# Attention and expert kernel on one Trainium2 core: the score exponential's factor, the engine that sends the maxima's rows, and a new plan

## The chip, the cores and the metric

The kernel runs on one core of a Trainium2 chip. The metric is the device time of one execution in microseconds (us); the time before is the median of three executions. The engines are TensorE (PE; its weight loads are PEld), VectorE (DVE), ScalarE (ACT), GpSimd (POOL) and SyncE (SP, which here only issues transfers).

## The reference, cut to what matters

```python
def attention(q, k, v, mask, ...):                  # q = layernorm(x), k = v = ctx
    qh, kh, vh = (heads(t @ W + b) for ...)         # 8 batches, 512 tokens, 16 heads of 32
    sim = einsum('bnid,bnjd->bnij', qh, kh) * 32 ** -0.5
    sim = where(mask, sim, finfo.min)
    return merge(einsum('bnij,bnjd->bnid', softmax(sim), vh)) @ Wo + bo

x = x + attention(layernorm(x), ctx, ctx, mask, ...)
x = x + experts(layernorm(x))   # softmax over 8 experts; each takes its 512 likeliest tokens,
                                # 512 -> 2048 -> 512 with gelu, weighted by the probability
```

The change concerns the attention only. If a batch's mask is false everywhere, every score of it is the same and the softmax is flat.

## The kernel before, in words

The attention works on 32 groups: four heads of one batch each, four groups to a batch, group g belonging to batch g // 4. All of it is fp32 or in high and low parts ("hi", "lo") that together carry fp32. For each group:

- **Projections** ("proj"): 12 matmuls for K and 12 for Q. ACT writes the rounded high part (L1271), DVE the rest (L1480). SP sends both to memory (`keep_hi`, `keep_lo`) and brings them back stacked by head (`stack_hi`, `stack_lo`), 256 KB each, into one of three stacks `kst`, `qst`. The queries' weights carry the factor -SCALE, so every product is a negated score.
- **Maxima** ("max"): 16 matmuls (L1906). DVE reduces each to its row's minimum, that is the negated maximum (L1495, `nmax`). ACT takes an exponential of each with scale -1 and the minimum as bias, for the sum of the row (L1294, "sum").
- **Rows** ("rows"): PE transposes the group's 16 columns of minima (L1923), ACT writes the negated high part `by_row` (L1285), DVE the low part (L1503), and POOL issues two transfers of 8 KB that put the two as rows below the queries in `qst` (L1188, "rows_lo").
- **Scores** ("score"): 16 matmuls, transposed, with the maxima's rows and the mask's row in the contraction (L1938). ACT takes the exponential into a ring of ten tiles (L1306), with `keep_scale[:, b]` as its factor: a column that holds -1 for a batch with a mask that is true somewhere and 0 for the others.
- **Attention** ("att"): after every eight exponentials 16 short matmuls (L1950); then the division and split, and after four groups the output projection, the residual, the second layernorm and the router of that batch.

Four times a batch a normalised tile of x is turned by PE (L1848), copied by ACT into `xT` (L1242, "turn") and its low part written by DVE (L1425, "turn_lo"). The context's tiles are split by ACT and DVE (L1251, L1431, "csplit").

The start is ordered by hand (`first_steps`): the mask is turned into the row that is added to the scores on DVE (L1444, "mask"), and `any` and `scale` make `keep_scale` later (L1447 to L1455). From there on a planner (`Plan.run`) orders the steps of every engine: it simulates them with the costs of `COST` (busy time and time until seen), picks on each engine, among the steps that could start within `LOOK` of the first, the one due first, and writes the orders out. The due times come from the tables `LAG`, `K_AT`, `Q_AT`, `MAX_AT`, `ROWS_AT` and their like, and `SPAN`. Each engine then runs its list in order, with semaphores for the dependencies. Seven PSUM banks (`ps_gen`) go round.

The experts' part after the attention is not touched.

Of the kernel before, what the change touches and what calls it, by code (L numbers as in the profile page):

```python
# [12 lines left out]
ALU = mybir.AluOpType  # L13
# [34 lines left out]
def raw(ap):  # L48
    return ap.bitcast(F32)
# [15 lines left out]
class Part:  # L65

    def __init__(self, engine, step, at, cost, after, line, takes, frees):
        self.engine, self.step, self.at = engine, step, at
        self.busy, self.seen = cost
        self.after, self.line = after, line  # L70
        self.takes, self.frees = takes, frees
        self.ready = None


class Plan:
# [14 lines left out]
    def run(self):  # L90
# [11 lines left out]
        def startable(part):  # L102
# [19 lines left out]
            if part.engine == "pe" and start > 0:  # L122
                start += 0.107
            return max(start, free[part.engine])

        left = len(self.parts)
        while left:
# [18 lines left out]
            part.start, part.ready = start, start + part.seen  # L146
# [14 lines left out]
class Agenda:  # L161
# [107 lines left out]
def first_steps(a):  # L269
# [15 lines left out]
    a.add("csplit", 0, 0)  # L285
    for t in range(TB):
# [38 lines left out]
    a.add("any")  # L325
# [13 lines left out]
    a.with_bank("scale")  # L339
# [4 lines left out]
    for n in range(AHEAD):  # L344
        if n in (0, AHEAD // 2):
# [12 lines left out]
    "act": {"proj": (0.585, 0.73), "sum": (0.662, 0.82), "rows": (0.174, 0.30), "score": (0.570, 0.72), "osplit": (0.613, 0.79),  # L358
            "csplit": (0.520, 0.66), "turn": (0.477, 0.64), "out": (0.570, 0.70), "logits": (0.157, 0.31), "route": (0.477, 0.64),
# [3 lines left out]
            "stats": (1.020, 1.10), "norm": (0.453, 0.57), "turn_lo": (0.598, 0.72), "outa": (0.600, 0.72), "out": (1.750, 1.80),  # L363
            "x1_norm": (0.453, 0.57), "route": (0.602, 0.72), "back": (0.300, 0.35), "choice_max": (0.330, 0.41),
            "choice": (0.540, 0.60), "wsplit": (0.660, 0.78), "tables": (0.500, 0.60)},
    "pool": {"rows_lo": (1.050, 3.20), "recip": (0.560, 0.66), "load": (0.550, 4.00), "load_wo": (0.550, 3.30),
             "residual": (0.550, 4.00), "stats": (0.600, 0.75), "add_bias": (1.240, 1.39), "out": (0.600, 0.75),
             "tables": (12.0, 12.0)},
    "sync": {"keep_hi": (0.360, 2.30), "keep_lo": (0.360, 2.30), "stack_hi": (0.800, 6.00), "stack_lo": (0.400, 5.50),
             "mask_row": (0.400, 2.50), "out": (0.360, 3.00), "x1_norm": (0.360, 3.00), "choice_out": (0.360, 2.50),  # L370
             "piece_in": (0.800, 3.00)},
}
STATISTICS = (1.020, 1.10)
LOOK = 0.0426
HELD = {"max": 3, "score": 2}
LAG = {
    ("act", "proj"): 0.05484, ("dve", "proj_lo"): 0.03444, ("pool", "rows_lo"): -1.2319, ("act", "rows"): 0.05934, ("dve", "rows_lo"): -0.39318,
    ("sync", "stack_hi"): -0.1324, ("sync", "stack_lo"): 0.32238, ("pool", "recip"): -0.22892, ("dve", "rden"): -0.10981, ("dve", "outa"): -0.55719,
    ("dve", "csplit_lo"): 0.14552, ("dve", "turn_lo"): 0.07169, ("dve", "v"): 0.09611, ("dve", "out"): 0.28314, ("act", "turn"): -0.1072,
    ("dve", "back"): -0.27443, ("act", "osplit"): -0.13848, ("dve", "divide"): 0.35342, ("act", "logits"): -0.65667, ("pool", "add_bias"): -0.4782,  # L380
    ("act", "csplit"): -0.41652, ("pe", "rows"): 0.31085, ("dve", "route"): -0.18136, ("dve", "max"): -0.08449, ("dve", "recip"): 0.36993,
    ("act", "score"): 0.06302, ("act", "sum"): 0.03381, ("pe", "score"): -0.37338, ("dve", "osplit_lo"): 0.16448, ("sync", "den_in"): 0.07696,
    ("sync", "den_out"): -0.05949, ("sync", "x1_norm"): -0.16445, ("sync", "mask_row"): 0.30337, ("sync", "out"): -0.0589,
}
K_AT = ((0.17737, 0.32917), (-0.06676, 0.27306), (0.03391, 0.12332), (-0.36248, 0.0798))
Q_AT = ((0.41689, 0.44452), (0.22572, 0.38938), (0.15766, 0.48119), (0.21384, 0.41343))
MAX_AT = ((-0.09122, 0.64471), (-0.04898, 0.72386), (0.03696, 0.90366), (0.22145, 0.759))
ROWS_AT, RECIP_AT, RDEN_AT, OSPLIT_AT, ATT_AT = -0.02924, 0.29201, 1.04897, -0.32083, -0.00839
SPAN = {
    "v": (-1, 0.31587, 1.56315), "load_c": (-3, 0.08839, 0.47212), "csplit": (-3, -1.07277, -0.68353), "load_x": (-3, 0.70493, 0.90564),  # L390
    "stats": (-3, 0.54052, 0.56032), "norm": (-3, 0.60153, 1.16671), "turn": (-3, 0.36103, 0.69481), "residual": (2, -0.18127, 0.43968),
    "add_bias": (2, 1.67672, 2.03871), "outa": (2, 0.23879, 1.06483), "out": (4, 0.09582, 0.86724), "x1_norm": (4, 0.44118, 0.9951),
    "route": (4, -0.06979, 1.17386), "logits": (4, 0.65291, 1.28237), "back": (4, 0.73224, 1.47973),
# [7 lines left out]
def attention_agenda():  # L401
# [48 lines left out]
    for g in range(NG):  # L450
# [22 lines left out]
        if g >= 1:  # L473
# [16 lines left out]
        for kt in range(KT):  # L490
            for h in range(HG):
                n = (g * KT + kt) * HG + h
                at = g + (kt + h / HG) / KT
                p.add("pe", ("score", g, kt, h), at, [("pool", "rows_lo", g)], takes=("score", g, kt, h))
# [76 lines left out]
def attention_moe_kernel(nc, x, ctx_T, mask, Wq, bq, Wk, bk, Wv, bv, Wo, bo,  # L571
# [9 lines left out]
    with ExitStack() as top:  # L581
# [261 lines left out]
        def stack_of(w, g):  # L843
            return (qst if w == "q" else kst)[g % NST]
# [1374 lines left out]
```

## Time and profile before

| | |
|---|---|
| time, median of 3 (lowest, highest) | 1653.58 us (1653.11, 1653.91) |
| span of the profiled execution | 1648.1 us |
| that execution's own time | not recorded; the median of the runs lies 5.5 us above the span |
| PE, PEld busy | 1581.2 us (96%), 1164.5 us (71%) |
| DVE busy | 1118.8 us (68%) |
| ACT busy | 979.2 us (59%) |
| POOL busy | 302.8 us (18%) |

The span runs from the first to the last instruction. "Busy" for PE counts each matmul from its start to a modelled end, and matmuls overlap, so its share is not the share of its best rate. The "chain that ended last" follows the last instruction back to what released it at every step. In it the time of a step runs from what released it to what it released, so that for an engine that works without a gap a piece divided by its count is the time from one start to the next. A transfer is listed under the engine that issues it (SPq, POOLq).

### The profile page before, as it was taken

Reading aid. Unit: us, or ns where it says so; the run is one execution under the profiler, and the core shown is the slowest. Engines: PE = TensorE matmul, PEld = TensorE weight load, DVE = VectorE, ACT = ScalarE, POOL = GpSimd, SP = SyncE. Lnnn points to the kernel's source line nnn. Section 1 sums busy time; section 2 is a strip of 40 time slices with the busy share of each in tenths; the row PEclk is TensorE's granted clock in tenths of the full one; section 3 lists DMA queues with packets and bytes.
Section 4 is the critical chain, followed back from the end, with each engine's and each line's share of the span. In section 5 each row is a group of like instructions: output and inputs, shape, how many; then the busy total and the mean of one; then the engine's idle time right before and its main releaser. Section 6 shows DMA issues by size and latency. Waiting matters only on the chain.

```text
span 1648.1 us, 22236 instructions
## 1 busy us (share of the span) xinstructions
PE 1581.2 (96%) x7826; PEld 1164.5 (71%) x7826; DVE 1118.8 (68%) x1976; ACT 979.2 (59%) x2119; POOL 302.8 (18%) x396
## 2 busy tenths in 40 slices
PE   7999999999999999999885999999999999999998
PEld 5657666676666766667543777888888888888886
DVE  7687978879788797887736688675554555454553
ACT  5899898998989989899863223222222223232321
POOL 6220321302213032130300201002020202020100
PEclk9999999999999999999988999999999999999999
DMA  5543644636446364463601433416253525333340
GB/s 180 178 137 105 204 143 136 187 106 204 142 136 187 106 203 142 138 185 110 205 36 65 129 102 96 142 52 186 77 160 103 160 78 159 103 103 134 99 131 26
DMA packets 131271, 217.26 MB, mean 132 GB/s; under 512 B 17117, under 2 KB 51057, under 8 KB 131161
## 3 DMA queue, kind: packets, MB, share of 16 engines
q1 hardware_dynamic: 114520, 173.23, 33.4%
q0 software_dynamic: 16640, 42.61, 9.9%
q8 instruction: 63, 1.03, 0.3%
q14 instruction: 48, 0.39, 0.1%
HBM read 157.45 MB, written 57.82 MB: 131 GB/s over the span
## 4 chain that ended last, share of the span: by engine, by line
PE 72%; DVE 13%; ACT 9%; DMA 3%; issue 2%; POOL 0%; SPq 0%; ACTq 0%; DVEq 0%; POOLq 0%
PE ps_gen L899 9%; PE ps_gen L900 9%; PE ps_gen L901 9%; PE ps_gen L2107 7%; PE ps_gen L2108 7%; PE ps_gen L2109 7%; PE ps_att L1950 5%; PE ps_gen L1938 4%; PE ps_gen L1906 4%; ACT ps_gen L1294 4%; ACT p_ring L1306 4%; DVE nmax L1495 4%; PE ps_gen L1888 2%; PE ps_gen L1889 1%; PE ps_gen L1890 1%
## 5 line engine op out<-in xcount | busy, mean ns | idle before, releaser
L1495 DVE TENSOR_REDUCE nmax<-ps_gen 128x1 f32<-128x512 f32 x512 | 329.6, 684 | 60.5 <-PE ps_gen L1906 59.8
L1294 ACT ACTIVATE ps_gen<-ps_gen,nmax 128x512 f32<-128x512 f32 x512 | 350.2, 695 | 24.5 <-DVE nmax L1495 24.1
L1306 ACT ACTIVATE p_ring<-ps_gen,keep_scale 128x512 f32<-128x512 f32 x512 | 343.7, 716 | 32.6 <-PE ps_gen L1938 28.7
L1368 ACT ACTIVATE gel<-ps_gen,b_cols 128x512 f32<-128x512 f32 x128 | 88.4, 690 | 446.3 <-PE ps_gen L901 434.1
L1770 DVE TENSOR_TENSOR gel_lo<-gel,gel_hi 128x512 fp32r<-128x512 f32 x126 | 87.3, 693 | 269.3 <-ACT gel_hi L1369 265.0
L899 PE MATMUL ps_gen<-hT_hi,w_hi 128*128 128x512 f32 x504 | 199.2, 395 | 0.0
L2107 PE MATMUL ps_gen<-w_hi,gel_hi 128*128 128x512 f32 x504 | 198.0, 393 | 0.0
L901 PE MATMUL ps_gen<-hT_hi,w_lo 128*128 128x512 f32 x504 | 196.4, 390 | 0.0
L2109 PE MATMUL ps_gen<-w_hi,gel_lo 128*128 128x512 f32 x504 | 196.4, 390 | 0.0
L900 PE MATMUL ps_gen<-hT_lo,w_hi 128*128 128x512 f32 x504 | 196.3, 390 | 0.0
L2108 PE MATMUL ps_gen<-w_lo,gel_hi 128*128 128x512 f32 x504 | 196.2, 389 | 0.0
L1938 PE MATMUL ps_gen<-qst,kst 99*128 99x512 f32 x512 | 192.2, 423 | 3.2 <-ACT p_ring L1306 2.3
L1906 PE MATMUL ps_gen<-kst,qst 97*128 97x512 f32 x512 | 184.3, 415 | 8.1 <-issue 6.0
L1216 POOL DMA_INDIRECT out_x<-y_out,idx x28 | 48.7, 1739 | 508.9 <-ACT y_out L1388 502.5
L1938 PEld LDWEIGHTS ps_gen<-qst,kst 99*128 99x128 f32 x512 | 93.8, 190 | 62.8 <-issue 33.5
L1906 PEld LDWEIGHTS ps_gen<-kst,qst 97*128 97x128 f32 x512 | 96.6, 189 | 58.4 <-issue 26.9
L1950 PE MATMUL ps_att<-p_ring,v_sb 128*32 128x512 f32 x1024 | 127.6, 617 | 4.2 <-ACT p_ring L1306 3.9
L1294 ACT ACTIVATION_READ_ACCUMULATOR ps_gen<-ps_gen,nmax 128x1 f32 x512 | 122.8, 240 | 0.0
L901 PEld LDWEIGHTS ps_gen<-hT_hi,w_lo 128*128 128x128 f32 x504 | 94.6, 188 | 20.2
L2109 PEld LDWEIGHTS ps_gen<-w_hi,gel_lo 128*128 128x128 f32 x504 | 94.6, 188 | 19.7
L2107 PEld LDWEIGHTS ps_gen<-w_hi,gel_hi 128*128 128x128 f32 x504 | 94.8, 188 | 19.3
L899 PEld LDWEIGHTS ps_gen<-hT_hi,w_hi 128*128 128x128 f32 x504 | 94.6, 188 | 19.3 <-issue 0.2
(233 smaller groups left out, 2699.9 us busy)
## 6 DMA issues: line engine op xcount, KB each, us to landing
w_raw<-in_L_ffn_W SPq DMA_DIRECT2D x128, 512.0 KB, 5.2
kst<-qk_rows SPq DMA_DIRECT2D x93, 256.0 KB, 3.9
qst<-qk_rows SPq DMA_DIRECT2D x93, 256.0 KB, 3.7
x_in<-in_x POOLq DMA_DIRECT2D x60, 256.0 KB, 4.0
out_x<-x_in SPq DMA_DIRECT2D x32, 256.0 KB, 2.3
qk_rows<-kT_hi SPq DMA_DIRECT2D x31, 256.0 KB, 2.2
qk_rows<-kT_lo SPq DMA_DIRECT2D x31, 256.0 KB, 3.5
qk_rows<-qT_hi SPq DMA_DIRECT2D x31, 256.0 KB, 2.0
```

The costliest lines, as they stand in the source:

```text
L899: e.matmul(psum, lhsT=wh, rhs=mh, start=(i == 0), stop=False)
L900: e.matmul(psum, lhsT=wh, rhs=ml, start=False, stop=False)
L901: last = e.matmul(psum, lhsT=wl, rhs=mh, start=False, stop=(i == n - 1))
L1294: e.activation(psum[:, :], psum[:, :], ACT.Exp, bias=nmax[g % 2][:, c], scale=-1.0, accum_out=den[g % 2][:, c]).then_inc(drained_sem("max" ...
L1306: e.activation(p_ring[n % NP_][:, :], ps("score", g, kt, h)[:, :], ACT.Exp, scale=keep_scale[:, b:b + 1]).then_inc(drained_sem("score", g, ...
L1495: e.tensor_reduce(nmax[g % 2][:, h * TB + t:h * TB + t + 1], ps("max", g, h, t)[:, :], AX.X, ALU.min).then_inc(s_min, 1)
L1906: e.matmul(ps("max", g, h, t)[:, :], lhsT=qst[k][0:ROWS_MAX, h, t * P:(t + 1) * P], rhs=kst[k][0:ROWS_MAX, h, :], start=True, stop=True).t ...
L1938: e.matmul(ps("score", g, kt, h)[:, :], lhsT=kst[k][0:ROWS_ALL, h, kt * P:(kt + 1) * P], rhs=qst[k][0:ROWS_ALL, h, :], start=True, stop=Tr ...
L1950: last = e.matmul(ps_att[h * DH:(h + 1) * DH, :], lhsT=v_sb[:, kt, (c4 * HG + h) * DH:(c4 * HG + h + 1) * DH], rhs=p_ring[((g * KT + kt) * ...
L2107: e.matmul(ps_y[tt], lhsT=gh, rhs=wh, start=(j == 0), stop=False)
L2108: e.matmul(ps_y[tt], lhsT=gh, rhs=wl, start=False, stop=False)
L2109: return e.matmul(ps_y[tt], lhsT=gl, rhs=wh, start=False, stop=(j == NF - 1))
```

## The change

1. The score exponential takes the constant factor -1.0. What `keep_scale` did moves ahead: `keep`, a column of 1 or 0 for each batch, scales `xT` (the factor of ACT's copy L1242, and a fused multiply and subtract on DVE for the low part), and the queries' bias (`bias_q`, one small product at the start). The mask's row is multiplied by the same flag. The small steps of `any` move into "mask", the first step of DVE, and `scale` to right after the first of `csplit`.
2. ACT issues the two transfers of the maxima's rows as a step of its own, `rows_out`; POOL's `rows_lo` is gone.
3. The planner's model: a transfer has a third cost, the time it moves, and all transfers of a plan pass one after the other (`moved`); POOL's transfers get a wake-up time. Costs of score, turn, turn_lo and all transfers are new, and so are `LOOK` and all due times. Queues of the chip that the transfers use are not altered by this, apart from point 2.

```diff
@@ Plan.run
+            if part.engine == "pool" and part.moving:
+                start += POOL_WAKE
...
-            part.start, part.ready = start, start + part.seen
+            if part.moving:
+                moved = max(moved, start + UNDER_WAY) + part.moving
+            part.start, part.ready = start, (moved if part.moving else start) + part.seen
@@ first_steps
     a.stats(0, 0)
     a.add("csplit", 0, 0)
+    a.with_bank("scale")
...
-    a.add("any")
@@ COST (excerpt)
-    "act": score (0.570, 0.72), turn (0.477, 0.64)
+    "act": score (0.477, 0.63), turn (0.570, 0.73), rows_out (0.700, 0.64, 0.88)
-    "dve": turn_lo (0.598, 0.72)
+    "dve": turn_lo (0.660, 0.78)
-    "pool": rows_lo (1.050, 3.20), load (0.550, 4.00)
+    "pool": load (0.550, 1.32, 1.02)
-    "sync": keep_hi (0.360, 2.30), stack_hi (0.800, 6.00), stack_lo (0.400, 5.50), out (0.360, 3.00)
+    "sync": keep_hi (0.360, 0.65, 0.76), stack_hi (0.800, 1.21, 2.36), stack_lo (0.400, 1.21, 1.18), out (0.360, 0.65, 0.81)
+UNDER_WAY, POOL_WAKE = 0.63, 0.52
-LOOK = 0.0426
+LOOK = 0.02907
@@ due times (excerpt)
-K_AT = ((0.17737, 0.32917), (-0.06676, 0.27306), (0.03391, 0.12332), (-0.36248, 0.0798))
+K_AT = ((-0.18058, 0.20097), (0.03196, 0.24309), (-0.90506, 0.5657), (0.4388, 0.8197))
-ROWS_AT, RECIP_AT, RDEN_AT, OSPLIT_AT, ATT_AT = -0.02924, 0.29201, 1.04897, -0.32083, -0.00839
+ROWS_AT, RECIP_AT, RDEN_AT, OSPLIT_AT, ATT_AT = -10.12924, -0.99724, 1.09785, -5.58345, 0.24374
-    "csplit": (-3, -1.07277, -0.68353), "stats": (-3, 0.54052, 0.56032), "norm": (-3, 0.60153, 1.16671), "turn": (-3, 0.36103, 0.69481)
+    "csplit": (-3, -5.99308, -2.39779), "stats": (-3, 1.26308, 2.17968), "norm": (-3, 2.08446, 2.10771), "turn": (-3, -6.93587, -3.59742)
@@ gpsimd_program: kind "rows_lo" removed; scalar_program:
+                elif kind == "rows_out":
+                    g, = at
+                    k = g % NST
+                    on.wait_ge(s_nmax_hi, g + 1)
+                    on.wait_ge(*drained("rows", g))
+                    for r in range(2):
+                        dst = qst[k][ROWS_MAX + r:ROWS_MAX + r + 1, :, :].rearrange("p h (t n) -> p (h t) n", n=P)
+                        e.dma_start(raw(dst), raw(max_rows[r])).then_inc(s_maxrow[k], 16)
@@ turn (ACT)
+                    on.wait_ge(*drained("scale"))
-                                 ACT.Copy).then_inc(s_turn_hi, 1)
+                                 ACT.Copy, scale=keep[:, b:b + 1]).then_inc(s_turn_hi, 1)
@@ score (ACT)
-                    on.wait_ge(*drained("scale"))
-                                 scale=keep_scale[:, b:b + 1]).then_inc(drained_sem("score", g, kt, h), 1)
+                                 scale=-1.0).then_inc(drained_sem("score", g, kt, h), 1)
@@ turn_lo (DVE)
-                    e.tensor_tensor(lo[:, :, cols], ps("turn", b, t)..., raw(hi[:, :, cols]), ALU.subtract)
+                    on.wait_ge(*drained("scale"))
+                    e.scalar_tensor_tensor(lo[:, :, cols], ps("turn", b, t)..., keep[:, b:b + 1],
+                                           raw(hi[:, :, cols]), ALU.mult, ALU.subtract)
@@ mask (DVE)
-                    e.tensor_scalar(mask_neg, mask_u8, 1.0, -MASKED, ALU.subtract, ALU.mult).then_inc(s_mask, 1)
+                    e.memset(ones_b, 1.0).then_inc(s_any, 1)
+                    e.reduce_max(mask_any[:, 0:1], mask_u8, AX.X).then_inc(s_any, 1)
+                    on.wait_ge(s_any, 2)
+                    e.tensor_scalar(mask_any[:, 1:2], mask_any[:, 0:1], -MASKED, None, ALU.mult).then_inc(s_any, 1)
+                    on.wait_ge(s_ident, 2)
+                    e.tensor_scalar(mask_diag, ident[0:B, 0:B], mask_any[:, 0:1], None, ALU.mult).then_inc(s_any, 1)
+                    on.wait_ge(s_any, 3)
+                    e.tensor_scalar(mask_neg, mask_u8, 1.0, mask_any[:, 1:2], ALU.subtract, ALU.mult).then_inc(s_mask, 1)
```

## Rows read from the trace of the kernel before

**Rows 1.** Windows over one batch and the last stage, busy time of each engine.
```profile
core 0: us, PE busy (x) PEld busy (x) DVE busy (x) ACT busy (x) POOL busy (x), PEclk, DMA share, GB/s
186.00:208.00 22.00, 21.33 (x111) 14.06 (x114) 21.52 (x50) 22.00 (x53) 9.05 (x16) 1.00 0.77 221
208.00:226.00 18.00, 17.83 (x87) 12.16 (x80) 13.86 (x23) 17.71 (x43) 5.34 (x5) 1.00 0.55 158
226.00:289.00 63.00, 62.62 (x345) 42.32 (x345) 48.51 (x93) 54.89 (x130) 8.86 (x16) 1.00 0.43 131
```

**Rows 2.** Chain over the whole span: start us, us, what, how many.
```profile
205.06 1.20 DVE xT_lo L1425 x2
...
719.67 1.20 DVE xT_lo L1425 x2
```

**Rows 3.** Chain pieces of PE at full rate.
```profile
345.05 0.70 PE ps_gen L1906 x3
345.76 1.85 PE ps_att L1950 x16
...
374.72 1.02 PE ps_gen L1981 x8
...
800.86 0.35 PE ps_gen L1992 x8
```

**Rows 4.** Groups of PE by line and shape, 186 to 289 us.
```profile
L1906 PE MATMUL ps_gen<-kst,qst 97*128 97x512 f32 x64 | 23.1, 413 | 0.2 <-issue 0.2
```

**Rows 5.** The page's chain by line, share of the span.
```profile
PE ps_gen L899 9%; PE ps_gen L900 9%; PE ps_gen L901 9%; PE ps_gen L2107 7%; PE ps_gen L2108 7%; PE ps_gen L2109 7%; PE ps_att L1950 5%; PE ps_gen L1938 4%; PE ps_gen L1906 4%; ACT ps_gen L1294 4%; ACT p_ring L1306 4%; DVE nmax L1495 4%; PE
```

**Rows 6.** Groups of ACT, 100 to 780 us: busy, mean ns of one.
```profile
L1294 ACT ACTIVATE ps_gen<-ps_gen,nmax 128x512 f32<-128x512 f32 x427 | 291.9, 695 | 13.6 <-DVE nmax L1495 13.3
L1306 ACT ACTIVATE p_ring<-ps_gen,keep_scale 128x512 f32<-128x512 f32 x426 | 284.6, 715 | 15.8 <-PE ps_gen L1938 12.3 <-PE ps_att L1950 3.3
...
L1242 ACT ACTIVATE xT_hi<-ps_gen 128x512 fp32r<-128x512 f32 x24 | 14.4, 600 | 0.2
```

**Rows 7.** Chain pieces of ACT and DVE, start to start.
```profile
57.09 1.16 ACT p_ring L1306 x2
...
98.24 0.97 ACT xT_hi L1242 x2
...
395.60 0.66 DVE kT_lo L1480
```

**Rows 8.** Timeline of the rows' transfers of one group, and an issue by SP.
```profile
202.35 0.25 ACT L1285 ACTIVATE by_row<-ps_gen 16x128 fp32r<-16x128 f32 x1
...
203.15 0.28 DVE L1503 SCALAR_TENSOR_TENSOR by_row<-ps_gen,by_row 16x128 fp32r<-16x128 f32 x1
...
204.11 1.04 POOL L1188 DMA_DIRECT2D qst<-by_row  x2
...
788.14 0.43 SPq L1001 DMA_DIRECT2D qst<-qk_rows  x1
```

**Rows 9.** Transfers issued, 100 to 780 us: KB each, us to landing.
```profile
qst<-by_row POOLq DMA_DIRECT2D x54, 8.0 KB, 1.7
...
hn_rows<-probs SPq DMA_DIRECT2D x6, 16.0 KB, 3.7
```

**Rows 10.** Timeline of the start.
```profile
2.39 1.22 DVE L1444 TENSOR_SCALAR att_n<-hnT 8x512 f32<-8x512 uint8 x1 [2.39 <-DMA hnT<-in_mask_BxS_bf]
...
8.28 0.69 DVE L1399 BATCH_NORM_STATS2 stat<-x_in 128x6 f32<-128x512 f32 x1 [0.63 <-DMA x_in<-in_x]
```

**Rows 11.** Chain pieces of the start.
```profile
31.06 0.56 DVE mask_any L1448
...
31.64 2.58 DVE hnT L1451
```

**Rows 12.** Timeline of the last batch's rows.
```profile
794.24 0.28 DVE L1503 SCALAR_TENSOR_TENSOR by_row<-ps_gen,by_row 16x128 fp32r<-16x128 f32 x1
...
795.69 1.12 POOL L1188 DMA_DIRECT2D qst<-by_row  x2
```

More of the change, by code:

```diff
@@ L68, in __init__ @@
         self.engine, self.step, self.at = engine, step, at
-        self.busy, self.seen = cost
+        self.busy, self.seen, self.moving = cost if len(cost) == 3 else (*cost, 0.0)
         self.after, self.line = after, line
@@ L192, in flush @@
             self.add(*step)
+            if step[0] == "rows_lo":
+                self.add("rows_out", *step[1:])
             if step[0] == "proj_lo" and step[2] > 0:
@@ L357 @@
            "out": (1.395, 1.60), "route": (0.436, 0.63), "logits": (0.405, 0.52), "back": (0.109, 0.31)},
-    "act": {"proj": (0.585, 0.73), "sum": (0.662, 0.82), "rows": (0.174, 0.30), "score": (0.570, 0.72), "osplit": (0.613, 0.79),
-            "csplit": (0.520, 0.66), "turn": (0.477, 0.64), "out": (0.570, 0.70), "logits": (0.157, 0.31), "route": (0.477, 0.64),
+    "act": {"proj": (0.585, 0.73), "sum": (0.662, 0.82), "rows": (0.174, 0.30), "score": (0.477, 0.63), "osplit": (0.613, 0.79),
+            "rows_out": (0.700, 0.64, 0.88), "csplit": (0.520, 0.66), "turn": (0.570, 0.73), "out": (0.570, 0.70), "logits": (0.157, 0.31), "route": (0.477, 0.64),
             "choice_exp": (0.136, 0.26), "wsplit": (0.585, 0.72)},
@@ L372 @@
 }
+UNDER_WAY, POOL_WAKE = 0.63, 0.52
 STATISTICS = (1.020, 1.10)
-LOOK = 0.0426
+LOOK = 0.02907
 HELD = {"max": 3, "score": 2}
 LAG = {
[L377 to L383, printed above, removed]
-}
@@ new lines @@
+    ("sync", "stack_hi"): 7.66529, ("sync", "stack_lo"): -3.25076, ("pool", "recip"): -5.85126, ("dve", "rden"): 5.74093, ("dve", "outa"): -4.90526,
+    ("dve", "csplit_lo"): -4.62331, ("dve", "turn_lo"): -6.03831, ("dve", "v"): 0.35238, ("dve", "out"): 9.60795, ("act", "turn"): 3.44102,
+    ("dve", "back"): -1.55549, ("act", "osplit"): -12.44774, ("dve", "divide"): 1.99703, ("act", "logits"): -0.04355, ("pool", "add_bias"): -2.55963,
+    ("act", "csplit"): -2.00333, ("pe", "rows"): 1.86319, ("dve", "route"): 1.38391, ("dve", "max"): 0.85937, ("dve", "recip"): 9.20098,
@@ new lines @@
+    ("act", "score"): 0.01787, ("act", "sum"): 0.14054, ("pe", "score"): -0.448, ("dve", "osplit_lo"): -0.00517, ("sync", "den_in"): 2.04378,
+    ("sync", "den_out"): -0.82492, ("sync", "x1_norm"): 8.96442, ("sync", "mask_row"): 4.39681, ("sync", "out"): -4.5904,
+}
+K_AT = ((-0.18058, 0.20097), (0.03196, 0.24309), (-0.90506, 0.5657), (0.4388, 0.8197))
+Q_AT = ((0.35617, 0.3775), (0.56137, 0.60155), (-0.23227, 0.99298), (-0.16533, 0.25259))
+MAX_AT = ((-0.15614, 0.68273), (-0.17985, 0.94047), (0.18874, 0.26582), (0.13739, 0.73499))
@@ L393 @@
-    "route": (4, -0.06979, 1.17386), "logits": (4, 0.65291, 1.28237), "back": (4, 0.73224, 1.47973),
+    "v": (-1, 0.88131, 1.31374), "load_c": (-3, -4.98761, -3.19799), "csplit": (-3, -5.99308, -2.39779), "load_x": (-3, -3.37841, -2.10456),
+    "stats": (-3, 1.26308, 2.17968), "norm": (-3, 2.08446, 2.10771), "turn": (-3, -6.93587, -3.59742), "residual": (2, -3.26548, -2.34535),
+    "add_bias": (2, 2.53614, 2.75803), "outa": (2, -0.71101, 1.78355), "out": (4, 0.0329, 0.77707), "x1_norm": (4, 1.45684, 5.86106),
@@ L394 @@
+    "route": (4, -5.39973, -2.43408), "logits": (4, 0.92452, 1.46148), "back": (4, -0.37717, 0.41803),
 }
@@ L493, in attention_agenda @@
                 at = g + (kt + h / HG) / KT
-                p.add("pe", ("score", g, kt, h), at, [("pool", "rows_lo", g)], takes=("score", g, kt, h))
+                p.add("pe", ("score", g, kt, h), at, [("act", "rows_out", g)], takes=("score", g, kt, h))
                 p.add("act", ("score", g, kt, h), at,
```

71 lines of the change are left out of this document (31 added, 40 removed).

## The prediction

> **What bounds the kernel now.** I read the windows first. In the experts' part nothing changes, so the case is the attention, and there one batch repeats. The turn of x's tiles comes back at 205.06 us and, five batches later, at 719.67 us [rows 2]: a period of (719.67 - 205.06) / 5 = 102.9 us. The reader is to see three stages in it [rows 1]. From 186 to 208 us DVE works 21.52 of 22 us and ACT all of them; this is where the next batch's statistics, normalisation, turn and splits fall together. From 208 to 226 us ACT works 17.71 of 18 us and DVE 13.86. In the other 63 us both have room (48.51 and 54.89 us), and PE sets the pace.
>
> PE's busy share (95% to 99%) hides its losses, because matmuls overlap. So I count what a period would take at PE's full rate. The groups by line give 64 maxima [rows 4], as many scores, 96 projection matmuls, 48 for v and 48 for the output: 320 of 512 columns. The chain shows three in 0.70 us, 0.233 each, the sixteen of an attention step in 1.85 us, eight transposes in 1.02 us and eight small router matmuls in 0.35 us [rows 3]. So 320 x 0.233 + 8 x 1.85 + 56 x 0.1275 + 32 x 0.044 = 74.6 + 14.8 + 7.1 + 1.4 = 97.9 us. The period loses 5.0 us to ACT and DVE. Seven such periods hold 35 us; that is the most which a better order with less work on ACT can win there, beside the start and the last batch.
>
> **The change part by part.**
>
> *Scores with an immediate factor.* L1306 has one column operand, its factor, and takes 715 ns; L1294 has one too, its bias, and takes 695; L1242 copies as many elements out of PSUM with none, in 600 [rows 6]. From start to start it is 1.16 / 2 = 0.58 us against 0.97 / 2 = 0.485 [rows 7]. So a score should fall by 0.095 us. What the rows leave open is whether the difference lies in the operand or in the function (a copy is no exponential); that bounds the gain by 0 and 0.095 us for each of 512. I take 0.095, since the bias-fed exponential and the factor-fed one cost nearly alike and the copy alone has no operand. A sentence aside: the Trainium skill (ScalarE: Activation LUTs, "What ACT_TABLE_LOAD costs") says that each column operand adds about 93 ns whatever the function; by that rule the same term is 512 x 0.093 = 47.6 us of ACT's time, and the trace's 0.095 agrees with it.
>
> What of it lies on the path? The chain gives L1306 4% of 1648.1 us [rows 5], 66 us, so 66 / 0.58 = 114 of the 512. Term 1: -114 x 0.095 = -10.8 us. The other 398 hide behind PE, DVE or the sums.
>
> *The factor on x instead.* ACT's turn copy gets the operand that the score loses: 32 x 0.095 = 3.0 us of ACT, off the chain in the steady state, where DVE's half is on it (two of L1425 in 1.20 us [rows 2]). That becomes a fused multiply and subtract with a column operand, as L1480 is: 0.66 us for 0.60 [rows 7]. Term 2: +32 x 0.06 = +1.9 us, all counted because this stage is DVE's. Bounds 0 and +4.9 (both halves).
>
> *Rows sent by ACT.* The trace has no transfer issued by ACT. The nearest row is SP's issue of 0.43 us; POOL takes 1.04 us for the two [rows 8]. I take SP's lower neighbourhood, 0.35 each: 0.7 us a group, 22 us in all, between nothing on the path and 32 x 1.04 = 33 us. ACT alone sets the pace in 18 of 103 us [rows 1]; the pair falls there by chance. Term 3: 22.4 x 18 / 103 = +3.9 us. What waits behind it: every sum and score in ACT's list, and through them PSUM banks and PE. ACT also waits for DVE's low half. In the group shown ACT's high half starts at 202.35 and DVE's ends at 203.43 us [rows 8], 0.8 us after ACT's own end. Before, ACT put two other steps in between; the new list can too, so I take 0. A transfer lands 1.7 us after its issue from POOL, one of 16 KB from SP after 3.7 [rows 9]; POOL's began 0.68 us after DVE was done [rows 8]. I take the landing as unchanged. For the last batch POOL was late: DVE was done at 794.52, and POOL, behind a residual's addition, issued at 795.69 [rows 12], on the chain. Term 4: -1.0 us (0 to -1.2). Aside: the Trainium skill (DMA: Bandwidth & Descriptors, "Issuing engines are not separate DMA queues") speaks against more: moving a transfer to another engine saves only sequencer time, and all share sixteen engines. By it the landing stays what it is and the sum too; the trace has no such transfer to confirm it.
>
> *The start.* `any` stood on the chain: 0.56 us for the reduction and 2.58 us for a product of 8x8 elements [rows 11], far too long for its size. It stands beside POOL's work on the v weights, and the next DVE step may inherit the delay: the removal gives 0.6 to 3.1 us. The steps come back ahead of the first statistics, about 1 us after the mask's 1.22. There DVE still waits for x's third tile, 0.63 us up to 8.28 [rows 10], which hides that much of it; without that cover all of it shows. I take the middle of the gain, 1.9, and nothing for the rest of the delay. Term 5: -1.9 us (-3.1 to +0.4).
>
> Sum of these: -10.8 + 1.9 + 3.9 - 1.0 - 1.9 = -7.9 us.
>
> *The new orders.* The trace cannot show them. What it shows is what they can win. Terms 1 to 3 recover about 0.6 of the 5.0 us that a period loses, so 4.4 x 7 = 31 us are left, and most of that loss is the pile of DVE work from 186 to 208 us. The new due times ask for csplit and turn as soon as they can start and make statistics and normalisation late, which turns them into filling for DVE's gaps (48.51 of 63 us busy next door). Against it, DVE has no work less, and an order which fits a model can be wrong by tenths of a us on each step. I take a quarter of what is left. Term 6: -8 us (31 / 4), between -31 (PE never waits) and +20 (0.6 us more lost in each of 32 groups).
>
> Total: -16 us. The span goes to 1648.1 - 16 = 1632.1 us. With the 5.5 us that lie between the span and the median of the runs, 1637.6 us; I say 1638.
>
> **The rivals.**
>
> *A, relief swallowed, no change.* ACT gets faster but DVE and PE hold the stages: then term 1 counts only where ACT alone is full [rows 1], 512 x 18 / 103 = 89 scores, -8.5 us, and terms 2 and 3 give 5.8 back: 1653.6 - 2.7 = 1651 us, with no gain of order. For: in 186 to 208 us DVE alone would fill the time. Against: ACT too is full there.
>
> *B, slower: ACT stands at `rows_out`.* Its list is fixed, so when DVE's low half comes late, ACT idles where before it was POOL that waited. The price is the 0.8 us of [rows 8] a group, and 1.4 with one more DVE step of 0.6 us ahead of it; ACT is full in 40 of 103 us [rows 1], which is the share that I let reach the path. With 1.4 us and no gain of order: 1653.6 - 8 + 32 x 1.4 x 0.39 = 1663 us. It decides from (8 + 3.3) / (32 x 0.39) = 0.9 us a group. For: the new due time makes ACT take the step as soon as the plan lets it. Against: the plan knows the dependency and PE's banks give slack.
>
> *C, the order does nearly all.* PE is held only by itself in most of a period: half to all of term 6's 31 us, 1653.6 - 8 - 24 = 1622 us. For: the loss sits in one 40 us stretch and the neighbouring engine time is free. Against: csplit can't begin before the last K projection of the batch, so part of the pile stays.
>
> *D, a wrong model of transfers.* The plan counts a stack as landed sooner; if maxima are put ahead of it PE waits in order. 31 groups at 0.7 us: 1653.6 - 8 + 22 = 1668 us. Against: the chain has transfers in it only at the start and in the last batch.
>
> **How the numbers follow.** Forecast (its own range 1629 to 1649 us) 0.46, C 0.22, A 0.14, B 0.11, D 0.07. Below 1616 there is 1 in 20 (PE at its full rate nearly everywhere); above 1657, from B and D, some 3 in 20. The range is 1616 to 1657. Two runs of this kernel differ by less than 0.2% (3.3 us), which I use as the bound of no change. Faster takes the forecast, C and a fifth of A: 0.71. Same 0.12. Slower, B and D nearly whole: 0.17.
>
> **What would show it.** Right: the score's mean near 0.62 us; 64 transfers from ACT's queue, some 0.35 us each, landing in about 1.7 us; ACT's busy time near 979 - 49 + 3 = 933 us; a period of 101 to 102 us; the stage in which DVE is full shorter than 22 us; nothing of DVE at 31 us on the chain. Wrong: scores at 0.7 us; idle time of ACT ahead of `rows_out` in every group (B); PE waiting for stack transfers in the steady state (D); a period still at 102.9 (A) or under 100 (C).

## The result and the profile after

The changed kernel takes 1663.88 us (median of 4 runs, 1661.85 to 1665.52), the kernel before 1653.74 in the same rounds: a ratio of 1.0058 with a 95% interval of 1.0044 to 1.0073. It is slower by 10 us, where I forecast 16 us faster. All medians below are taken beside runs of the kernel before, whose medians lay between 1653.5 and 1654.4 us. In every run whose span is on record the time is 1.7 to 2.0 us above the span, not 5.5: so the profiled execution of the kernel before, with its span of 1648.1 us, was a quick one of about 1650 us (an estimate from these two numbers), and the two traces lie 14.2 us apart where the medians lie 10.1.

The page of the changed kernel: the span, busy time by engine, and the chain by engine.

```profile
span 1662.3 us, 22253 instructions
...
PE 1581.0 (95%) x7826; PEld 1173.2 (71%) x7826; DVE 1120.3 (67%) x1978; ACT 943.5 (57%) x2119; POOL 265.8 (16%) x332
...
PE 73%; DVE 9%; ACT 7%; DMA 7%; issue 2%; ACTq 1%; POOL 0%; SPq 0%; DVEq 0%; POOLq 0%
```

Its groups of ACT between 100 and 780 us, which answer to [rows 6].

```profile
L1317 ACT ACTIVATE p_ring<-ps_gen 128x512 f32<-128x512 f32 x414 | 234.1, 605 | 50.2 <-PE ps_gen L1953 29.6 <-PE ps_att L1965 9.7 <-issue 8.4
...
L1247 ACT ACTIVATE xT_hi<-ps_gen,keep 128x512 fp32r<-128x512 f32 x24 | 14.5, 688 | 8.7 <-issue 8.7
```

The reader is to see that the relief came as forecast: a score takes 605 ns for 715 and ACT is busy 35.7 us less. But ACT now stands idle 50.2 us ahead of its scores, where it was 15.8 [rows 6]. Part of that is only the shorter score (in e9 below, the fastest kernel, it is 34.3 us); the rest is ACT being fed late. On the chain transfers have grown to 7%.

One line of the scores' matmuls says who feeds them late. First the changed kernel's rows' transfers, all 64 of them, then the same kernel's table of waits, 100 to 780 us (us, times, longest).

```profile
L1298 ACTq DMA_DIRECT2D qst<-by_row x64: 510/606/1357, 44.9 to 864.1; - x64
...
  PE ps_gen L1953: 21.6, 9
...
DMA to landing us min/median/max: 1.8/1.9/6.2
```

```profile
PE ps_gen L1953 <- DMA qst<-by_row: 17.9, 7, 3.6
```

The median landing is 1.9 us, hardly more than the 1.7 of [rows 9]. The maximum is what counts: once a batch the second of the two small transfers needs 5.4, 5.5, 6.2, 6.1, 5.3 and 4.7 us, and PE waits. In the kernel before, at the same place of the batch, it was 2.6, 2.4, 4.0, 3.2, 2.5 and 3.1 us, and PE did not wait for it. Pieces of the chain of the changed kernel:

```profile
176.63 7.30 DMA x_in<-in_ctx
...
198.06 1.60 DVE x_in L1419 x4
...
200.92 5.38 DMA qst<-by_row
...
305.58 5.50 DMA qst<-by_row
...
412.18 6.17 DMA qst<-by_row
```

Its timeline around the first of these shows what they share the way with.

```profile
200.00 0.28 DVE L1518 SCALAR_TENSOR_TENSOR by_row<-ps_gen,by_row 16x128 fp32r<-16x128 f32 x1
...
200.36 1.11 POOL L1132 DMA_DIRECT2D x_in<-in_x  x2 [3.34 <-PE ps_gen L1863]
...
200.36 1.17 ACTq L1298 DMA_DIRECT2D qst<-by_row  x2
...
200.44 0.78 SPq L1003 DMA_DIRECT2D kst<-qk_rows  x2
...
202.02 1.06 POOL L1132 DMA_DIRECT2D x_in<-in_x  x2
...
206.43 0.75 PE L1953 MATMUL ps_gen<-qst,kst 99*128 99x512 f32 x2 [2.75 <-DMA qst<-by_row]
```

ACT starts to issue 0.08 us after DVE has written the low half, and so it does in each of the 32 groups: ACT's list has always come to `rows_out` by then and stands at it. But in all 32 groups together the engine was idle for only 2.5 us between the step before and the issue. Within 0.1 us of the issue POOL issues the first of four loads of 256 KB, and SP asks for K's stack (two transfers). In the kernel before the same transfers were spread out, around the rows at 204.11 [rows 8]:

```profile
203.42 0.70 POOL L1119 DMA_DIRECT2D x_in<-in_x  x1 [3.24 <-PE ps_gen L1848]
...
205.14 1.11 POOL L1119 DMA_DIRECT2D x_in<-in_x  x2
...
205.76 0.79 SPq L990 DMA_DIRECT2D kst<-qk_rows  x2
```

One load went just ahead of the rows, the other three behind them in POOL's own list, and the stack 1.65 us behind them by SP's. So two things changed for the rows: the loads no longer stand behind them in one list, and the new plan starts K's stack only 0.21 us, and the first load 0.25 us, behind the rows (the starts that the planner of the changed kernel writes down, the same in six batches).

The wait costs more than its own length. Windows of the changed kernel, in the columns of [rows 1]:

```profile
204.00:206.00 2.00, 0.00 (x0) 0.00 (x0) 1.62 (x3) 0.67 (x2) 1.26 (x1) 1.00 0.99 291
206.00:208.00 2.00, 1.57 (x7) 1.46 (x8) 0.00 (x0) 1.06 (x2) 0.00 (x0) 0.74 0.75 299
208.00:210.00 2.00, 2.00 (x7) 1.52 (x6) 1.50 (x4) 1.10 (x4) 0.00 (x0) 0.50 0.32 117
210.00:212.00 2.00, 2.00 (x9) 1.63 (x8) 0.84 (x2) 1.61 (x6) 1.99 (x3) 0.91 0.00 0
```

PE stands for the whole of 204 to 206 us, and just behind it the granted clock is 0.50, the lower of the two levels (1.2 GHz of 2.4); the chain's matmuls go from 0.23 to 0.43 us each. In these four windows (0.26 + 0.50 + 0.09) x 2 = 1.7 us are lost that way, where the windows of before stand at 1.00 [rows 1], beside 2.75 us of waiting. Another stop, of 1.9 us up to 185.4 us, stands behind the context load of 7.30 us above, and the clock is 0.62 and 0.53 in the two windows from 186 to 190. From 100 to 780 us such low windows cost 11.9 us in the changed kernel and nothing before (each window counted as above). In the same stretch PE stands idle 28.2 us (its busy time there is 651.8 of 680 us), against 8.4 before. The two together are 31.7 us, more than the 14.2 us by which the spans differ: the new lists and the shorter score win some 17 us elsewhere, and the stops and the clock take them back and more.

### The profile page after: what moved, and what is told of

The parts are those of the page before. It is cut to its first block, busy times and chain, and to the rows that moved or that the text cites. A ratio compares the mean times of both kernels' runs of the same rounds, so it can differ in the third digit from the quotient of the medians.

```text
span 1662.3 us, 22253 instructions
## 1 busy us (share of the span) xinstructions
PE 1581.0 (95%) x7826; PEld 1173.2 (71%) x7826; DVE 1120.3 (67%) x1978; ACT 943.5 (57%) x2119; POOL 265.8 (16%) x332
## 4 chain that ended last, share of the span: by engine, by line
PE 73%; DVE 9%; ACT 7%; DMA 7%; issue 2%; ACTq 1%; POOL 0%; SPq 0%; DVEq 0%; POOLq 0%
PE ps_gen L912 9%; PE ps_gen L914 8%; PE ps_gen L913 8%; PE ps_gen L2122 7%; PE ps_gen L2124 7%; PE ps_gen L2123 7%; PE ps_gen L1953 5%; PE ps_gen L1921 4%; PE ps_att L1965 4%; ACT ps_gen L1307 4%; DMA qst<-by_row 3%; DVE nmax L1510 2%; ACT p_ring L1317 2%; PE ps_gen L1903 2%; PE ps_gen L1904 2%
## 5 line engine op out<-in xcount | busy, mean ns | idle before, releaser
L1307 ACT ACTIVATE ps_gen<-ps_gen,nmax 128x512 f32<-128x512 f32 x512 | 342.8, 674 | 31.1 <-DVE nmax L1510 26.1
L1317 ACT ACTIVATE p_ring<-ps_gen 128x512 f32<-128x512 f32 x512 | 289.9, 608 | 66.7 <-PE ps_gen L1953 43.2
L1953 PE MATMUL ps_gen<-qst,kst 99*128 99x512 f32 x512 | 193.6, 427 | 22.3 <-DMA qst<-by_row 21.6
L1307 ACT ACTIVATION_READ_ACCUMULATOR ps_gen<-ps_gen,nmax 128x1 f32 x512 | 111.6, 218 | 0.0
L914 PEld LDWEIGHTS ps_gen<-hT_hi,w_lo 128*128 128x128 f32 x504 | 94.6, 188 | 20.4
L2123 PEld LDWEIGHTS ps_gen<-w_lo,gel_hi 128*128 128x128 f32 x504 | 94.7, 188 | 19.1
```

The source lines that it names most:

```text
L914: last = e.matmul(psum, lhsT=wl, rhs=mh, start=False, stop=(i == n - 1))
L1307: e.activation(psum[:, :], psum[:, :], ACT.Exp, bias=nmax[g % 2][:, c], scale=-1.0, accum_out=den[g % 2][:, c]).then_inc(drained_sem("max" ...
L1317: e.activation(p_ring[n % NP_][:, :], ps("score", g, kt, h)[:, :], ACT.Exp, scale=-1.0).then_inc(drained_sem("score", g, kt, h), 1)
L1953: e.matmul(ps("score", g, kt, h)[:, :], lhsT=kst[k][0:ROWS_ALL, h, kt * P:(kt + 1) * P], rhs=qst[k][0:ROWS_ALL, h, :], start=True, stop=Tr ...
L2123: e.matmul(ps_y[tt], lhsT=gh, rhs=wl, start=False, stop=False)
```

## The experiments

A period is taken as in [rows 2], but from PE's transposes of the minima: one group's start, and the one five batches later.

| kernel | median us | ratio, 95% interval | starts, period us | mean clock, profiled execution |
|---|---|---|---|---|
| before | 1653.7 | 1 | 102.9 | 0.990 |
| changed | 1663.88 | 1.0058 [1.0044, 1.0073] | 198.65, 732.64: 106.8 | 0.984 |
| e1 | 1647.36 | 0.9961 [0.9947, 0.9974] | 201.86, 714.21: 102.5 | 0.990 |
| e2 | 1684.59 | 1.0187 [1.0165, 1.0209] | | 0.989 |
| e3 | 1692.77 | 1.0222 [1.0190, 1.0254] | | 0.979 |
| e4 | 1679.25 | 1.0153 [1.0128, 1.0177] | | 0.981 |
| e5 | 1655.27 | 1.0010 [0.9998, 1.0021] | 201.38, 716.65: 103.1 | 0.989 |
| e6 | 1646.95 | 0.9962 [0.9943, 0.9981] | 197.37, 710.81: 102.7 | 0.991 |
| e7 | 1663.07 | 1.0045 [1.0025, 1.0065] | | 0.983 |
| e8 | 1642.46 | 0.9930 [0.9912, 0.9947] | 197.42, 708.26: 102.2 | 0.990 |
| e9 | 1630.19 | 0.9859 [0.9845, 0.9874] | 220.11, 719.31: 99.8 | 0.990 |
| e10 | 1643.53 | 0.9935 [0.9922, 0.9948] | 197.56, 712.05: 102.9 | 0.991 |
| e11 | 1634.44 | 0.9886 [0.9869, 0.9904] | 196.71, 707.40: 102.1 | 0.991 |
| e12 | 1647.49 | 0.9958 [0.9943, 0.9973] | 201.82, 714.79: 102.6 | 0.988 |

**e1, the factor alone.** The old planner and lists; the constant factor, `keep` on x, `bias_q` and the steps of the start as in the change; rows still sent by POOL.

```diff
 # kernel before
-    scale=keep_scale[:, b:b + 1]).then_inc(drained_sem("score", g, kt, h), 1)
+    scale=-1.0).then_inc(drained_sem("score", g, kt, h), 1)
```

> The kernel before with the immediate factor alone (point 1 of the change; old planner, old due times, rows still sent by POOL, so every list but the start's is the old one). It tests terms 1, 2 and 5 of the prediction, -10.8 + 1.9 - 1.9. All theories: 1653.7 - 10.8 = 1643 us, score mean near 0.605 us. If the relief is swallowed (rival A) 1650 to 1653.

Measured: 1647.36 us, 6.3 less. Its scores take 601 ns, and the start hides the new steps: the product of the mask takes 0.47 us for 1.22 [rows 10], and DVE still waits for x behind it. The gain of the start did not come, though: with `any` gone from 31 us the chain runs through ACT's sums there, ACT's high half of the next queries follows, and DVE's low half of it starts at 38.30 us where it was 37.70 before. The minima of the third group are turned at 99.9 us in both. The timeline of e1:

```profile
3.22 0.47 DVE L1455 TENSOR_SCALAR att_n<-hnT,mask_any 8x512 f32<-8x512 uint8 x1
```

**e2, the factor and rows by ACT, with the old costs and due times.** The plan is made anew, since the step sits on another engine.

```diff
 # e1
-            p.add("pool", ("rows_lo", g), at, [("dve", "rows_lo", g)])
+            p.add("act", ("rows_out", g), at, [("dve", "rows_lo", g)])
```

> Points 1 and 2 with the old planner and old due times (rows_out gets the due time and the landing time that POOL's rows_lo had). Theory 1, the rows' transfers collide with the residual loads because POOL's list no longer puts them ahead: a transfer of the rows of over 5 us once a batch and some 2 to 4 us lost each time, so 15 to 25 us above the kernel with the factor alone, about 1665. Theory 2, the new plan (its due times or its model of transfers) makes the loss by itself: within 5 us of the kernel with the factor alone, about 1647. Theory 3, ACT stands at its own transfers: 10 us above it with ACT idle ahead of them in every group.

**e3, all but the rows.** The new planner, costs and due times, with the rows on POOL in the plan.

```diff
 # changed kernel
-            p.add("act", ("rows_out", g), at, [("dve", "rows_lo", g)])
+            p.add("pool", ("rows_lo", g), at, [("dve", "rows_lo", g)])
```

> The changed kernel with the rows sent by POOL again (points 1 and 3; the planner's costs, model and due times of the changed kernel, POOL's rows with its costs). Theory 1: the loss is gone, 1640 us or less, no rows' transfer over 4 us on the chain. Theory 2: still slow, 1658 to 1668. Theory 3: 1650.

**e4, the changed kernel with the old `LOOK` and due times.**

```diff
 # changed kernel
-LOOK = 0.02907
+LOOK = 0.0426
-K_AT = ((-0.18058, 0.20097), ...
+K_AT = ((0.17737, 0.32917), ...
```

> The changed kernel with LOOK and all due times of the kernel before (points 1 and 2 and the new costs and model of transfers). Theory 1: as slow as the changed kernel, 1660 to 1668. Theory 2 with the due times at fault: 1645. Theory 2 with the model of transfers at fault: 1660 or more, PE waiting for stacks or rows.

Measured: 1684.59, 1692.77 and 1679.25 us, 37, 45 and 15 us above e1, e1 and the changed kernel. No theory of mine had expected e2 and e3; e4 falls in an open "1660 or more", but PE does not wait there for stacks or rows: its longest stops (3.1, 2.4 and 3.4 us) end with ACT's sums. These three don't tell the parts apart, since each made a plan that nobody had fitted. What a plan made anew costs can be read once e5 and e6 below stand beside them: e2 and e5 make the same change to the same kernel, e2 with a new plan and e5 with the lists kept, and lie 29.3 us apart; e3 and e6 in the same way 45.8. So from here on the lists are kept step for step and only the one step is moved.

**e5, the old lists, the rows moved to ACT's.**

```diff
 # e1, after the plan is made
+    for g in range(1, NG):
+        start = p.parts[("pool", "rows_lo", g)].start
+        a.order["pool"].remove(("rows_lo", g))
+        later = next(part for part in act if part.start >= start)
+        a.order["act"].insert(a.order["act"].index(later.step), ("rows_out", g))
```

> The factor alone, with that kernel's lists kept step for step, except that the rows' transfers move out of POOL's list into ACT's, to the planned time at which POOL sent them. The kernel with the factor alone took 1647.4 us, the same with rows by ACT and a plan made anew 1684.6. Theory 4, what costs is any plan made anew with due times that were fitted to another plan, and ACT as sender is harmless: 1645 to 1652, term 3 of the prediction (+3.9) at most. Theory 1, ACT as sender is the loss (its transfers collide or its list stands): 1660 or more.

Measured: 1655.27 us, +7.9 against e1. Its timeline at one pair, and the rows' transfers as a whole:

```profile
203.28 0.53 ACTq L1298 DMA_DIRECT2D qst<-by_row  x1
...
203.84 0.61 ACTq L1298 DMA_DIRECT2D qst<-by_row  x1
```

```profile
  PEld ps_gen L1953: 0.8, 1
...
DMA to landing us min/median/max: 1.8/1.9/5.0
```

A pair holds ACT from 203.28 to 204.45, about 1.15 us, not 0.7. The move alone makes the rows land a little later at this place (the second transfer in 3.4 to 4.6 us, 2.2 to 4.7 in e1), but the old lists have room for it: PE waited 0.8 us for a landing in the whole run. So next to nothing of the 7.9 us is landing, and I put them down to the issuing; 7.9 / (32 x 1.15) = 21% of it reaches the end, near the 18 / 103 that I had read off the windows. The result lies between the two theories, 3 us above the range of the fourth.

**e6, the new lists, the rows moved back to POOL's.** The mirror of e5.

```diff
 # changed kernel, after the plan is made
+    for g in range(1, NG):
+        start = p.parts[("act", "rows_out", g)].start
+        a.order["act"].remove(("rows_out", g))
+        later = next(part for part in pool if part.start >= start)
+        a.order["pool"].insert(a.order["pool"].index(later.step), ("rows_out", g))
```

> The changed kernel with its lists kept step for step, except that the rows' transfers move from ACT's list into POOL's at the planned time. Theory 1 with ACT's queue at fault: the long landings (5 to 6 us once a batch) go and the time falls to 1645 to 1650. Theory 5, the transfers share the engines in fact while the plan lets them pass one after the other, so whoever sends the rows they land late: landings stay at 4 to 6 us once a batch and the time stays within 5 us of 1664, or a little above.

Measured: 1646.95 us, 16.9 less than the changed kernel and within 0.5 of e1. Two things follow. Moving the rows is the loss. And the new orders, with the rows sent as before, win nothing by the medians (the ten runs reach from 1640.6 to 1656.0 us, so 3 us either way are open). The time is what the first theory gave, the landings (3.8 to 4.1 us in five batches of six) are what the fifth gave. Its waits, 100 to 780 us, say that it was still held by landings:

```profile
PE ps_gen L1959 <- DMA qst<-by_row: 11.2, 8, 2.0
```

The longest is 2.0 us for 3.6. Of its five stops of 1.7 to 2.0 us the clock falls to 0.50 behind one alone, of 1.94 us up to 306.5 us; behind the longest, of 2.03 us up to 512.85 us, it stays at 1.00. So in the profiled execution, one of the quicker ones (1641.8 us), the clock costs 1.7 us between 100 and 780 us, for 11.9 in the changed kernel.

**e7, the loads behind the rows.** The changed kernel, where POOL's loads for the residual wait once a batch until the rows have landed.

```diff
 # changed kernel, POOL ahead of the load (e7)
+                    if ("pool", "residual", b, t) in agenda.behind:
+                        g = agenda.behind["pool", "residual", b, t]
+                        on.wait_ge(s_maxrow[g % NST], 32 * (g // NST + 1))
```

> The changed kernel in which POOL, in batches 1 to 6, waits with the four residual loads until the rows sent at the same moment have landed. Theory 5: the rows land in 3 to 4 us instead of 5.5 (K's stack is still under way beside them), and some 2 us a batch are won, 1650 to 1656, unless the residual then comes late. Theory 4 (the order itself, not the landings): no change, 1662 to 1667.

**e8, loads and K's stack behind the rows.** The same wait on SP as well.

```diff
 # e7, SP ahead of the transfer of stack_hi (e8)
+                    if ("sync", "stack_hi", w, g) in agenda.behind:
+                        n = agenda.behind["sync", "stack_hi", w, g]
+                        on.wait_ge(s_maxrow[n % NST], 32 * (n // NST + 1))
```

> As the one before, and SP also waits with K's stack until the rows have landed. Theory 5: rows land in 2 us and 3.5 us a batch are won, 1640 to 1650, unless the stack, which is now 2 us later, is itself waited for. Theory 4: 1662 to 1668.

Measured: e7 1663.07 (twelve runs, 1655.3 to 1672.9), e8 1642.46 us. In e7 the rows take 3.8 to 4.7 us beside the stack, and PE's waits for them fall from 17.9 to 9.1 us. But POOL's list stands while the load waits, and behind the load in that list is the copy of the reciprocals (`rden_wide`) that PE needs next. PE's waits of e7, 100 to 780 us, and POOL's timeline:

```profile
PE ps_gen L1954 <- POOL rden_wide L1159: 9.7, 6, 1.8
PE ps_gen L1962 <- DMA qst<-by_row: 9.1, 7, 2.1
```

```profile
204.34 1.11 POOL L1141 DMA_DIRECT2D x_in<-in_x  x2 [7.82 <-DMA qst<-by_row]
205.45 0.62 POOL L1159 COPY rden_wide<-rden 128x512 f32<-128x512 f32 x1
```

So e7 does not say that the loads do no harm to the rows: what they gave back, the new wait took for another step. In e8 the rows land in 1.9 us in four batches of six and in 2.7 in the others, as its chain shows:

```profile
199.69 1.86 DMA qst<-by_row
...
506.37 1.87 DMA qst<-by_row
```

Nothing but the two waits, and with them the order of transfers, differs between the changed kernel and e8, and it is worth 21.4 us. PE still waits 5.6 us for `rden_wide`.

**e9, rows by POOL and the stack behind them.** e6 with SP's wait of e8. It has both: no issue on ACT, and the order of transfers.

```diff
 # e6, SP ahead of the transfer of stack_hi (e9)
+                        on.wait_ge(s_maxrow[n % NST], 32 * (n // NST + 1))
```

> The changed kernel's lists with the rows sent by POOL (1647.0 us so far), and SP in addition waits with K's stack until the rows sent at the same moment have landed. If both causes are real and separate (late landings of a transfer that shares the engines; 1.15 us of ACT for each pair that it issues), this is the best of both: rows land in 2 us and ACT issues nothing, 1634 to 1640. If the landing was all, as the one with ACT as sender and everything behind it, 1640 to 1644. If the landing does not matter, 1647.

**e10, the changed kernel with K's stack alone behind the rows.**

```diff
 # changed kernel, SP (e10); POOL's loads don't wait
+                        on.wait_ge(s_maxrow[n % NST], 32 * (n // NST + 1))
```

> The changed kernel in which only K's stack waits for the rows, and POOL's residual loads do not. The loads waiting alone gave 1663, both 1642.5. If the stack is the transfer that delays the rows: 1640 to 1646 and landings of 2 to 3 us. If it takes both to be out of the way: 1652 to 1660, landings near 4 us.

**e11, the rows sent by SP.** The new lists, the rows put into SP's list, so that they go out ahead of the stack without any wait.

```diff
 # changed kernel, after the plan is made
+        a.order["act"].remove(("rows_out", g))
+        later = next((part for part in sync if part.start >= start), None)
+        a.order["sync"].insert(at, ("rows_out", g))
```

> The changed kernel's lists kept, with the rows moved from ACT's list into SP's at the planned time, just ahead of K's stack in the same queue. ACT issues nothing. If a queue serves its own transfers in order, the rows land in 2 to 3 us with only POOL's loads beside them, and with the 37 us of ACT's issuing gone the time is 1638 to 1645. If SP, which now stands until DVE has made the rows, holds its stores back, 1650 to 1665.

Measured: 1630.19, 1643.53 and 1634.44 us: e9 and e11 quicker than any of their ranges, e10 within its first one. The timeline of e9 where the changed kernel stopped:

```profile
198.23 0.28 DVE L1533 SCALAR_TENSOR_TENSOR by_row<-ps_gen,by_row 16x128 fp32r<-16x128 f32 x1
...
199.09 1.03 POOL L1216 DMA_DIRECT2D qst<-by_row  x2 [3.33 <-DVE by_row L1533]
...
200.12 1.12 POOL L1147 DMA_DIRECT2D x_in<-in_x  x2
...
201.34 0.78 SPq L1018 DMA_DIRECT2D kst<-qk_rows  x2
...
201.84 0.73 PE L1968 MATMUL ps_gen<-qst,kst 99*128 99x512 f32 x2
```

The rows go first, the loads 1 us behind and the stack when the rows have landed, and the matmul starts 2.75 us behind the rows' issue with no wait for them (6.07 in the changed kernel). Between 122.53 and 775.82 us the chain of e9 holds no rows' transfer. PE's waits for them, 100 to 780 us, in e10 and then in e9:

```profile
PE ps_gen L1962 <- DMA qst<-by_row: 6.8, 7, 1.7
```

```profile
PE ps_gen L1968 <- DMA qst<-by_row: 3.1, 3, 1.8
```

From the changed kernel to e10, one wait on SP's queue gives 20.4 us; from e6 to e9 the same wait gives 16.8. In e10 the rows still land in 3.2 to 4.4 us beside the loads, not in the 2 to 3 that I had expected: the stack and the loads each delay them, and either alone leaves about 4 us. In the profiled executions PE's idle time between 100 and 780 us falls by 11.8 us from the changed kernel to e10 and the clock's loss by 11.9; the spans lie 20.1 us apart. With ACT's issuing left in, e8 and e10 stand 12.3 and 13.3 us above e9. That is the price of the issue in the new lists, at most: e9 also orders the loads otherwise, all four behind the rows. In e11 SP issues the same two transfers in 0.58 us each (median of 64), hardly less than ACT's 0.61; POOL takes 0.50.

**e12, e9 with the score's factor from a column of -1.**

```diff
 # e9
-    scale=-1.0).then_inc(drained_sem("score", g, kt, h), 1)
+    scale=minus[:, 0:1]).then_inc(drained_sem("score", g, kt, h), 1)
```

> The fastest version so far (changed lists, rows by POOL, K's stack behind them; 1630.2 us) with the scores' factor taken from a column again, a column of -1, so that each of 512 exponentials takes 0.095 us more and nothing else changes. Term 1 as the prediction has it, 114 of them on the path: +10.8 us, 1641. In the old lists the factor alone gave only -6.3 with everything; if the new lists need ACT's room more, +15 to +30 us, 1645 to 1660. If the relief is swallowed, +2 to +5 us, 1632 to 1635.

Measured: 1647.49 us, +17.3 against e9. The group of its scores, 100 to 780 us:

```profile
L1335 ACT ACTIVATE p_ring<-ps_gen,minus 128x512 f32<-128x512 f32 x427 | 284.4, 720 | 21.7 <-PE ps_gen L1971 11.1 <-PE ps_att L1983 9.7
```

The operand alone makes 720 ns of 610 (e9), which answers what I had left open between operand and function. The factor is worth 6.3 us in the old lists, with the start in it, and 17.3 in the new with the stack held back: these can use ACT's time.

## Why the prediction was wrong, point by point

- **What bounds the kernel** stands, and e9 bears it out: its period of 99.8 us is 1.9 above the 97.9 that I had worked out for PE at its full rate, where before lost 5.0.
- **Term 1, the factor (-10.8):** right in kind, 0.110 us a score. The terms 1, 2 and 5 sum to -10.8 and e1 measured -6.3. Its trace shows no gain of the start (term 5), so terms 1 and 2, -8.9 by my sum, made about -6.3: the share on the path was too large for the old lists.
- **Term 2, the factor on x (+1.9):** not measured by itself. ACT's copy takes 688 ns for 600.
- **Term 3, rows by ACT (+3.9): the step that failed.** It has two faults. The size: I took 0.35 us an issue, beneath SP's row, and it is 0.53 to 0.61; a pair is 1.15 us and cost 7.9 us in the old lists, up to 12 or 13 in the new. SP's row was for another transfer; SP needs 0.58 us for these (e11), and POOL's 1.04 us for the two, my own upper row, was the row for the same transfer. The larger fault is the sentence "I take the landing as unchanged". It is unchanged alone (1.9 us) and not once a batch, where it is 4.7 to 6.2 for 2.4 to 4.0 before, and PE waits 17.9 us for it between 100 and 780 us. I had asked who is queued behind the step on the engine that it joins. I hadn't asked what had been queued behind it on the engine that it leaves: POOL's loads. Nor had I asked what another queue sends at that moment in the new lists: K's stack, 0.2 us behind the rows by the plan. Both delay them; e6, which puts the loads back behind the rows and leaves the stack, has 11.2 us of these waits, e10, which holds back the stack alone, 6.8, and e8, which holds back both, 0.3.
- **The skill's rule, beside it:** the Trainium skill (DMA: Bandwidth & Descriptors, "Issuing engines are not separate DMA queues") says that transfers of all engines run on the same sixteen DMA engines and interleave there. The runs agree: e8 and the changed kernel differ only in when the large ones go out, and the small ones take 1.9 to 2.7 us in the one and 4.7 to 6.2 in the other. I read the rule as "then the landing stays what it is", which it does not say: transfers that interleave can delay each other as soon as a move lets them overlap.
- **Term 4, the last batch (-1.0):** not told apart. The changed kernel's chain has a rows' transfer of 5.79 us there at 835.08, and the kernel before had one of 6.1 us at 820.2, so no gain is seen.
- **Term 5, the start (-1.9):** the new steps ahead of the statistics were hidden, as I took it, but the gain at 31 us did not come (see e1): with `any` gone ACT's sums were the chain there. The 2.58 us of the 8x8 product [rows 11] were hardly its own: it ended at 34.22 us, and the second of POOL's two fills of 32x2048 beside it at 34.19. In e1 the same product takes 0.27 us. That it was held up by POOL is my reading of these times; no run tried it.
- **Term 6, the orders (-8):** by themselves -0.4 us (e6 against e1). With the stack held back by a wait, -17.2 (e9 against e1), more than I gave. The planner lets transfers pass strictly one after the other, so its 0.2 us of lead for the rows is enough for them: it expects them landed 2.15 us after the start of their issue. In the changed kernel, where all go out together, they took 4.7 to 6.2 us, and the lead was worth nothing.
- **The rivals.** B had the right size (1663) and the wrong cause: ACT's idle time ahead of `rows_out` is 2.5 us in all 32 groups together, where I had priced 1.4 us in each. D was the nearest in kind: a wrong model of transfers, but in the rows that are overtaken and not in a stack counted as landed too soon. I had given it 0.07 of the chances, and its "against" was wrong as well: the chain of before has two transfers in the steady state, stores of `out_x` of 5.3 us at 172.9 and 5.2 us at 481.6. A falls with e12 (for e9's lists), C is what e9 nearly reaches once the order is enforced (1630 for my 1622).
- **What I left out altogether** is the clock. PE's stop of 2.75 us brings 1.7 us more at the lower level, and all such stretches between 100 and 780 us cost 11.9 us. e8, e9 and e10 have shorter stops at this place and a clock of 1.00 in the 10 us around it; e7, with no gain, loses 13.7 us to the clock. The length of one stop does not decide it: e6's two stops of 1.94 and 2.03 us went different ways. What else does, these runs don't show.

Left open: how the 16.9 us between the changed kernel and e6 divide into issuing and landing, since e6 changes both. In the two profiled executions (22.3 us apart) PE waits 6.7 us less for rows and 7.6 us less for steps of ACT (7.8 and 0.2 us between 100 and 780 us), and the clock takes 10.2 us less; which cause each fall of the clock belongs to is not shown. Not tried alone: the other stop of each batch, in which POOL holds the context's loads until a store of `hn_rows` is done (62.2 us of POOL's waiting in 20 waits between 100 and 780 us); it stays on the chain of the changed kernel and stands once on e9's, at 768 us, though POOL waits there nearly as long (49.7 us).

## What to carry to other kernels

When a small, urgent transfer moves to another issuing engine, look at what stood behind it in the queue it leaves, and at what the other queues send at the same moment: a shared list was an ordering, and it has to be put back by a wait or by another list (a wait on SP's queue for the stack gave 16.8 to 20.4 us here, sending the rows from SP ahead of the stack, which takes ACT's issues away as well, 29.4). Before a wait is added to a queue, look at what stands behind it there: POOL's wait in e7 held up a copy that PE needed, and gave nothing. To judge one part of a change to a planned kernel, keep the planned lists and move the one step; the same changes with a plan made anew, under due times fitted to something else, came out 29.3 and 45.8 us slower, more than any part was worth. Price a stop of PE with what the clock takes after it.

## What the runs showed of the hardware that I had not expected

- The same transfer of 8 KB holds the engine that issues it for 0.61 us on ACT, 0.58 on SP and 0.50 on POOL (medians of 64 in the changed kernel, e11 and e9); single ones take up to 1.36 us on ACT in the changed kernel. SP issues those of K's stack, 256 KB each, in 0.30 and 0.43.
- Two transfers of 8 KB land in 1.9 us alone, in 3.2 to 4.7 us beside either four loads of 256 KB or K's stack, and in 4.7 to 6.2 us beside both.
- Behind PE's stop of 2.75 us in the changed kernel the granted clock was 0.50 from 208 to 210 us; in e6 it was 0.50 from 308 to 310 us behind a stop of 1.94 us, and 1.00 from 513 to 515 us behind one of 2.03 us.
- The mask's product of 8x512 bytes took 1.22 us at 2.39 us in the kernel before and 0.47 at 3.22 us in e1. It got a column for a constant, but the cause is not shown: a fill by POOL runs beside it until 3.3 us in both, 0.93 us of it beside the slow product and 0.1 us beside the quick one.
